# Cross-attention masks moved from TensorE to VectorE in a decoder layer, with work handed to GpSimd and a new instruction order

## The reference

```
x = x + self_attention(layernorm(x), w_qkv, w_out)             # 16 heads of 16, windows of 128:
                                                               # each window sees itself (causal) and the one before
x = x + cross_attention(layernorm(x), ctx, mask; Wq..Wo, biases)  # 77 context keys, mask[1024, 77]: 0 is -inf
x = x + ffn(layernorm(x))                                      # int8 fake quantisation of inputs, weights, hidden (704)
```

## Time and profile before

| | us |
|---|---|
| three timed executions | 696.09, 699.87, 700.06 (median 699.87) |
| the profiled execution | 695.62 |
| its span, first to last instruction | 693.5 |
| TensorE, VectorE, ScalarE, GpSimd busy | 607.9, 519.1, 406.6, 166.1 |
| attention ends (last values product) | about 553 |
| feed-forward begins (first int8 tokens) | about 582 |

### The profile page before, as it was taken

How to read it: one execution, slowest core, us unless ns; L and a number is a source line. 1 busy time by engine, 2 the same in 40 slices (tenths; PEclk the granted TensorE clock), 3 DMA queues, 4 the chain that set the end, 5 groups by cost and what they waited for, 6 DMA issues and landing times.

```text
span 693.5 us, 19987 instructions
## 1 busy us (share of the span) xinstructions
PE 607.9 (88%) x8020; PEld 393.6 (57%) x8020; DVE 519.1 (75%) x985; ACT 406.6 (59%) x602; POOL 166.1 (24%) x213
## 2 busy tenths in 40 slices
PE   2799999999999999999999999999989843877395
PEld 2556575867665766566757656576646432333173
DVE  6698877877787677757866966686697476699677
ACT  3345666775675547556555476544545715999682
POOL 2014332431344301320441033220120001455200
PEclk9999999999999999999999999999999966999789
DMA  7644133562344344246324353443473320000024
GB/s 258 182 153 134 42 122 110 143 155 66 111 136 112 104 117 104 71 138 165 114 52 145 79 145 102 113 112 93 101 216 98 75 48 1 0 1 1 0 92 153
DMA packets 58554, 72.17 MB, mean 104 GB/s; under 512 B 23979, under 2 KB 35423, under 8 KB 58463
## 3 DMA queue, kind: packets, MB, share of 16 engines
q1 hardware_dynamic: 54783, 68.92, 35.6%
q10 hardware_dynamic: 3680, 1.97, 1.1%
HBM read 17.74 MB, written 4.72 MB: 32 GB/s over the span
## 4 chain that ended last, share of the span: by engine, by line
PE 59%; DVE 19%; issue 6%; SPq 6%; DMA 5%; ACT 4%; ACTq 0%; POOL 0%; DVEq 0%; POOLq 0%
PE banks L484 38%; PE banks L664 7%; DVE mneg L1098 5%; PE banks L584 4%; PE banks L675 4%; SPq L417 2%; DVE tops L1282 2%; PE banks L528 2%; PE banks L729 1%; SPq L435 1%; DVE big L1276 1%; SPq L412 1%; DVE parts L1264 1%; DVE mneg L1102 1%; DMA out_dram<-oTs 1%
## 5 line engine op out<-in xcount | busy, mean ns | idle before, releaser
L484 PE MATMUL banks<-big 96*128 96x77 bf16 (+3 forms) x1344 | 157.7, 238 | 8.2 <-DVE mneg L1102 2.7
L1098 DVE TENSOR_REDUCE mneg<-banks 128x4 f32<-128x640 f32 (+3 forms) x128 | 126.9, 1019 | 38.7 <-PE banks L593 38.2
L484 PEld LDWEIGHTS banks<-big 99*128 99x128 bf16 (+2 forms) x1344 | 101.9, 101 | 75.2 <-issue 30.1
L1379 POOL TENSOR_SCALAR_AFFINE_SELECT big<-big 128x512 f32<-128x512 f32 x96 | 65.5, 683 | 230.1 <-ACT big L900 229.4
L900 ACT ACTIVATE big<-banks 128x1024 f32<-128x1024 f32 x96 | 96.9, 1028 | 38.9 <-PE banks L484 38.6
L484 PE MATMUL banks<-xnT,weights 128*128 128x512 f32 x192 | 92.4, 611 | 0.2 <-DVE mneg L1098 0.2
L584 PE MATMUL banks<-big 96*32 96x160 bf16 (+3 forms) x1792 | 70.8, 257 | 0.9 <-DVE mneg L1098 0.4
L904 ACT ACTIVATE big<-banks 77x1024 f32<-77x1024 f32 x48 | 47.6, 1021 | 26.5 <-PE banks L484 24.5
L1102 DVE TENSOR_REDUCE mneg<-banks 128x8 f32<-128x616 f32 x64 | 49.3, 790 | 14.6 <-PE banks L484 14.1
L664 PE MATMUL banks<-big 128*17 128x256 f32 x768 | 57.0, 382 | 0.2 <-ACT oe L913 0.2
L729 PE MATMUL banks<-oe,weights 128*128 128x512 bf16 x192 | 47.7, 395 | 10.1 <-DVE big L1276 4.4
(11 more groups left out here) (159 smaller groups left out, 1191.1 us busy)
## 6 DMA issues: line engine op xcount, KB each, us to landing
big<-parts SPq DMA_DIRECT2D x285, 128.0 KB, 2.5
oc<-sums SPq DMA_DIRECT2D x16, 512.0 KB
oTs<-oe SPq DMA_DIRECT2D x64, 64.0 KB, 2.5
out_dram<-oTs SPq DMA_DIRECT2D x16, 256.0 KB, 2.2
xs<-in_x_dram SPq DMA_DIRECT2D x3, 1024.0 KB, 6.0
big<-oe SPq DMA_DIRECT2D x32, 64.0 KB, 2.4
oTx<-oe SPq DMA_DIRECT2D x32, 64.0 KB, 2.4
xs<-in_x_dram SPq DMA_DIRECT2D x2, 512.0 KB, 6.3
```

The source lines that it names most:

```text
L484: return e.matmul(to[0:w], k[:, 0:w], q, start=start, stop=stop, skip_group_check=True)
L1098: e.tensor_reduce(M.rearrange("p (h c) -> p h c", h=4)[:, :, c], pair(p).rearrange("p j (s n) -> p (j s) n", s=2)[:, :, 0:160 + 32 * (c % 4)],
L1379: e.affine_select(out=P[:, :, 0:128], in_=P[:, :, 0:128], compare_op=ALU.is_ge, fill=0.0, base=0, pattern=[[0, 4], [1, 128]], channel_mult ...
```

## The change

1. `maskt` becomes f32 and holds a cap: 3e38 where the mask keeps a key, 0 where it doesn't. The two identity products are gone from each cross `score`. A new step `keep` (letter H), on VectorE, takes the minimum of the exponentials and the cap, and `val` waits for it instead of for ScalarE. The masks of the maxima stay as they are.
2. The step `split`'s third part goes from VectorE to GpSimd.
3. `scale` goes from VectorE to GpSimd for 15 of the 16 jobs.
4. For the last job the sums don't go through DRAM. VectorE multiplies the inverted sums into two tiles of 512 columns (`broad`), which TensorE multiplies by a matrix of zeros and ones (`heads`, made once by GpSimd in `pick`); VectorE then scales `oT` by the two banks. `store` and `widen` of that job are gone.
5. `ORDER` is a new string.

```
@@ maskt, once
-                    e.tensor_copy(maskt[0:KX, :], bank(p).bitcast(BF16)[0:KX, :]).then_inc(d_mask, 1)
+                    e.tensor_scalar(maskt[0:KX, :], bank(p).bitcast(BF16)[0:KX, :], 0.0, BIG, ALU.is_equal, ALU.mult
+                                    ).then_inc(d_mask, 1)
@@ TensorE, score of a cross job
-                        keep = maskt[0:KX, j * 256:j * 256 + 256].rearrange("p (a n) -> p a n", a=1)
                         for z in range(2):
                             for i in range(2):
-                                whole(bank(p, z)[0:KX, i * 256:i * 256 + 256], xks[r][0:99, 2 * z + i, :],
-                                       qs[r][0:99, 2 * z + i, j * 256:j * 256 + 256], i == 0, False, KX)
-                            t = whole(bank(p, z)[0:KX, :].rearrange("p (i n) -> p i n", i=2), identb[0:KX, 0:KX],
-                                       keep.to_broadcast([KX, 2, 256]), False, True, KX)
+                                t = whole(bank(p, z)[0:KX, i * 256:i * 256 + 256], xks[r][0:99, 2 * z + i, :],
+                                          qs[r][0:99, 2 * z + i, j * 256:j * 256 + 256], i == 0, True, KX)
@@ TensorE, val of a cross job
-                        e.wait_ge(a_exp, n_of["score", job, g, j])
+                        e.wait_ge(d_keep, n_of["keep", job, g, j])
@@ VectorE
-                elif k == "split":
...
-                    e.tensor_tensor(P[:, 2, :], rem[:, rem_at[s[1:]], :], P[:, 1, :], ALU.subtract).then_inc(d_p2, 1)
+                elif k == "keep":
+                    _, job, g, j = s
+                    P = pt[pt_at[job, g, j]][0:KX, :].rearrange("p (i n) -> p i n", i=4)
+                    e.wait_ge(a_exp, n_of["score", job, g, j])
+                    e.wait_ge(d_mask, 2)
+                    e.tensor_tensor(P, P, maskt[0:KX, j * 256:j * 256 + 256].rearrange("p (a n) -> p a n", a=1).to_broadcast(
+                        [KX, 4, 256]), ALU.min).then_inc(d_keep, 1)
-                elif k == "scale":
...
+                elif k == "broad":
+                    e.wait_ge(d_inv, len(JOBS))
...
+                    e.tensor_tensor(grown[:, s[1] * 512:s[1] * 512 + 512].rearrange("p (j n) -> p j n", j=8),
+                                    ls[:, 1, :].rearrange("p (a n) -> p a n", a=1).to_broadcast([128, 8, 64]),
+                                    group[:, 8 * s[1]:8 * s[1] + 8].rearrange("p (j a) -> p j a", a=1
+                                                                              ).to_broadcast([128, 8, 64]),
+                                    ALU.mult).then_inc(d_broad, 1)
+                elif k == "scale" and s[1] == JOBS[-1]:
...
+                    for half in range(2):
+                        to = oT[kind][f][:, half * 512:half * 512 + 512]
+                        e.wait_ge(t_broad, half + 1)
+                        e.tensor_tensor(to, to, bank(at_bank["broad", half][0]), ALU.mult).then_inc(d_scale, 1)
@@ TensorE, new
+                elif k == "broad":
+                    e.wait_ge(p_pick, 3)
+                    e.wait_ge(d_broad, s[1] + 1)
+                    whole(bank(p), heads, grown[:, s[1] * 512:s[1] * 512 + 512], True, True).then_inc(t_broad, 1)
@@ GpSimd, new
+                elif k == "scale":
...
+                    e.wait_ge(land_r, 32 * (n + 1))
+                    for g in range(2):
+                        e.wait_ge(land_o[g], 64 * (n + 1))
+                    e.tensor_tensor(oT[kind][f], oT[kind][f], oc[:, :], ALU.mult).then_inc(p_scale, 1)
+                elif k == "split":
+                    _, job, z, blk = s
+                    e.wait_ge(a_p1, n_of[s])
+                    P = parts[:, z, :, blk * 512:blk * 512 + 512]
+                    e.tensor_tensor(P[:, 2, :], rem[:, rem_at[s[1:]], :], P[:, 1, :], ALU.subtract).then_inc(p_p2, 1)
```

More of the change, by code:

```diff
@@ L22 @@
 NEG = -1.0e30
+BIG = 3.0e38
 EPS = 1e-5
@@ L29 @@
 AT = {j: n for n, j in enumerate(JOBS)}
+LAST_SELF = [j for j in JOBS if j[0] == "s"][-1]
 UNITS = {"s": NC, "x": 4}
@@ L67, in streams @@
         "s": [("score",) + unit for unit in units],
+        "H": [("keep",) + unit for unit in units if unit[0][0] == "x"],
         "v": [("val", job, g, j, j == UNITS[job[0]] - 1) for job, g, j in units],
@@ L72, in streams @@
         "i": [("invert", job) for job in JOBS],
-        "d": [("store", job) for job in JOBS],
-        "w": [("widen", job) for job in JOBS],
+        "d": [("store", job) for job in JOBS[:-1]],
+        "w": [("widen", job) for job in JOBS[:-1]],
+        "b": [("broad", half) for half in range(2)],
+        "P": [("pick",)],
         "x": [("scale", job) for job in JOBS],
@@ L132 @@
 WIDE = {"turned": 2, "max": 2, "score": 2, "up": 2}
-NARROW = {"turnw", "turnc", "masks", "keys", "qk", "v", "xkeys", "turnm", "out", "wturn", "turnx", "down", "dsc", "peak"}
+NARROW = {"turnw", "turnc", "masks", "keys", "qk", "v", "xkeys", "turnm", "out", "broad", "wturn", "turnx", "down", "dsc", "peak"}
 def banks_of(steps, count_of):
@@ L168, in build @@
         ks = [ring[:, r, 1] for r in range(4)]
-        fourth = sb("fourth", [128, 1024], F32)
-        pt = [big[:, 16384 + 1024 * i:17408 + 1024 * i] for i in range(3)] + [fourth[:]]
+        more = sb("more", [128, 1024], F32)
+        pt = [big[:, 16384 + 1024 * i:17408 + 1024 * i] for i in range(3)]
+        pt += [more[:, 1024 * i:1024 * i + 1024] for i in range(NPT - 3)]
         rem = big[:, 19456:20480].rearrange("p (i n) -> p i n", i=2)
@@ L387, in run_sync @@
                     for part, ready, n in ((0, a_p0, n_of["qk", job, z, 1]), (1, a_p1, n_of["split", job, z, 1]),
[L388 removed]
+                                           (2, p_p2, n_of["split", job, z, 1]))[:1 if s == first_keys else 3]:
                         e.wait_ge(ready, n)
@@ L414, in run_sync @@
                     else:
-                        e.wait_ge(d_p2, n_of["split", job, z, 1])
+                        e.wait_ge(p_p2, n_of["split", job, z, 1])
                         for rr in range(6):
@@ L446, in run_sync @@
                     if AT[job]:
-                        e.wait_ge(d_scale, AT[job])
+                        e.wait_ge(p_scale, AT[job])
                     else:
@@ L681, in run_tensor @@
                     e.wait_ge(ld_wo, 32)
-                    e.wait_ge(d_scale, scale_n((kind, b, 0), 1))
-                    e.wait_ge(d_scale, scale_n((kind, b, 1), c // 4))
+                    for f in range(2):
+                        n = AT[kind, b, f]
+                        e.wait_ge(*((p_scale, n + 1) if n < len(JOBS) - 1 else (d_scale, c // 4 + 1)))
                     for i in range(2):
@@ L756, in build @@
                 n_cross[s[1:]] = seen_cross
-        def scale_n(job, half):
-            n = AT[job]
-            return n + 1 + (half if n == len(JOBS) - 1 else 0)
         ffn = [("peak", 0)]
@@ L1073, in run_vector @@
                                                ).then_inc(d_rem, 1)
-                elif k == "split":
-                    _, job, z, blk = s
-                    e.wait_ge(a_p1, n_of[s])
-                    before = prior(job, lambda j: z == 0 or j[0] == "s")
-                    P = parts[:, z, :, blk * 512:blk * 512 + 512]
-                    e.tensor_tensor(P[:, 2, :], rem[:, rem_at[s[1:]], :], P[:, 1, :], ALU.subtract).then_inc(d_p2, 1)
                 elif k == "xkeys":
```

87 lines of the change are left out of this document (54 added, 33 removed).

## The result

The changed kernel takes 717.13 us (median, 709.34 to 720.97); the kernel before, measured beside it, 699.00. The ratio is 1.0226 with a 95% interval of [1.0184, 1.0269]: **slower by 2.3%**, where 684 us was forecast. The highest of the four runs after was in the slow state and counts in the median, but not in the ratio, so the loss is 16 us by the ratio and 18 by the medians. The profiled execution took 716.34 us (span 714.6), 20.7 over that of before.

A forecast was written before the change was run, and what follows sets the result against it. TensorE was taken to bound attention, VectorE its tail after the change. Start -3, middle -10, tail +6 and end -5, together -12 from the profiled 695.62 us, gave 684 us, range 667 to 702.

The forecast's parts named there:

- 212 to 455 us: Attention while own and cross jobs alternate: TensorE still bounds, 14.1 us less masks, 4 back for contention and later selects: -10.
- The tail, +6 (0 to +12): Only-cross attention, 455 to 553 us: VectorE becomes the bound with 99 us of work at 93% busy, +6 us.
- the first rival: All hidden: VectorE's 25 idle us of the tail take the minimums without loss, tail -10, 668 us; chance 0.18.
- VectorE's relief: 48 third-part subtractions (-32 us) and 15 scalings (-17 us) leave VectorE; GpSimd gets +61 and +38 us.
- The start: Until 212 us: VectorE -17.5 us, TensorE unchanged, slower splits take some back: -3 us (bounds -8 and +2).
- Part 4, the holds: VectorE and GpSimd operations with two SBUF inputs wait for each other: 11 us more on VectorE (bounds 0 and 41).
- The third rival: GpSimd and VectorE shut each other out at minimums and selects: 714 us, chance 0.12; sign: minimums' mean over 1.4 us.
- The Trainium skill's rule: GpSimd's SBUF interfaces are shared with VectorE, with contention for two SBUF inputs; the forecast said it speaks against this change.
- my second rival: Given back in the tail: tail +12, middle -5, start 0, end -4, TensorE's clock lower there: 699 us; chance 0.17.
- Casts' mean up from 317 ns: Sign in the profile after: the mean time of VectorE's casts rises from 317 ns.
- I am wrong if the mixed part doesn't shorten: Sign against the forecast: attention with alternating own and cross jobs, until 455 us, gets no shorter.
- The end, -5: Last sums through two products instead of DRAM: first out product at 560 instead of 565.01, -5 us (bounds -1 and -5.5).

The follow-up runs named there:

- half minimum: The change with each minimum on 77x512, half its columns, the other half unmasked, against the kernel before: 701.08 us, 1.0035.
- masks back: The change with its score masks back on TensorE and no minimum, splits and scalings still on GpSimd, against the kernel before: 704.59 us, 1.010.
- experiment 2: Parts of the change written into the old order, against the kernel before: end products 699.24 us, with third parts and scalings on GpSimd 708.94, all four parts 779.11.
- experiment 3: Idle VectorE work, shorter minimums or shared masks in the change's order, against the kernel before: idle minimums 718.93 us, half minimums 701.08, shared masks 703.28.
- load-only version: The change with masks on TensorE and an idle same-shape VectorE minimum in each minimum's place, nothing waiting for it, against the kernel before: 718.93 us, 1.0247.

## Why the prediction was wrong, step by step

- **The step that failed: "212 to 455 us ... TensorE still bounds; 14.1 less 4 for contention and later selects: -10".** Measured +11.3, which is 21 of the 33 us between forecast and result. Two terms of it failed. The 4 us for GpSimd's part was too small: with all masks on TensorE the move and the order cost 7.0 in the middle (5.8 for the move in the old order). And the 14.1 of relief didn't come: putting the masks on VectorE cost another 4.3. VectorE's busy time came out near the sum (192.0 against 185 and the holds), but I took 81% of a stage for "not the bound", while in jobs of 20 to 35 us it is full. With half the minimums' load the same relief of TensorE gives 7.8 us in the middle, so it can be had only while VectorE has room.
- **The tail, +6 (0 to +12).** Right in kind, a little over the upper bound in size, 12.2. VectorE bounds it (104.55 us of 110.3, 95%; 99 of work were forecast at 93%). "25 idle us of the tail" is what the first rival counted on: the half minimums found room for 22 us at a net price of 1.6 over masks back, the full ones, 37 us, cost 9.0.
- **VectorE's relief.** I counted 48 third parts and 15 scalings off VectorE as gains of its time and put little on GpSimd's side. In the old order they cost 9 to 10 us. The start came out at +2.4 in place of -3, and at +3.8 without minimums; GpSimd's queue does that rather than the order, which is likely from experiment 2, but not shown, since the new order doesn't stand VectorE in GpSimd's place. (The -17.5 of the start is 18.4 by its own terms, 22 x 0.68 and 3 x 1.15; nothing hangs on it.)
- **Part 4, the holds.** Normalisations rose by little (26.2 to 27.5 us) and casts fell (10.2 to 9.5), the minimums carry 7.5 us over 64 x 1.21: about 8 in place of 11. The third rival's sign, a mean over 1.4 us, did not show (1.33). Its 714 came near the measured time, but it asked for 0.36 us uncovered per minimum, and the holds are 0.12: luck in the number, not its mechanism.
- **The Trainium skill's rule** in "GPSIMD Engine Reference", section 1, that the SBUF interfaces are shared: the trace agrees, with 3.06 us in place of 1.21 for a minimum in a meeting. I used it for the price of the operations and not for the queue behind them.
- **The clock**, in my second rival, showed: between 212 us and the last mark its mean is 0.92 over 369.5 us, some 60 us at the half level, against 1.00 before. In the tail it costs little: the half minimum has a tail with 0.83 that is 7 us shorter. In the stretch from 287 to 349 us, where VectorE doesn't bound, it may be a part of the 5 us that experiment 3 finds; no run separates it from the link.
- **Signs:** GpSimd at 1.2 and 2.4 us, VectorE full in the tail with TensorE at 78%, and values products waiting for minimums (14.0 us in 11 waits) were right. "Casts' mean up from 317 ns" was wrong: it is 296. "I am wrong if the mixed part doesn't shorten": it didn't.
- **The end, -5.** Measured -4.9 behind the last mark, but that is luck. In the old order the products alone changed nothing (0.9991 to 1.0027), though the reciprocal behind the tiles made mark to end 131.5 us in place of 139.0: the mark moved, not the end. From the end of the last values product to the first out product I forecast 7 us in place of 12; it is 10, as the timeline of TensorE after shows (588.37 - 577.35 - 1.06). Two prices were missed: GpSimd's scaling of the job before holds the first multiply (2.26 us in place of 0.66), which I had only as a bound, and the two products take 3.75 us at the half clock, where I had 0.9 to 1.7. Another 2.3 us lie behind the first out product (128.5 us to the span's end before, 126.2 now).

```profile
577.35 1.06 PE L685 MATMUL banks<-more,big 77*17 77x256 f32 x8 [0.77 <-DVE more L1113]
584.47 3.75 PE L497 MATMUL banks<-big 128*128 128x512 f32 x4 [3.19 <-DVE big L1146]
588.37 0.75 PE L497 MATMUL banks<-weights,big 128*128 128x256 f32 x2
```

```profile
580.76 3.02 POOL L1411 TENSOR_TENSOR big<-big,oc 128x1024 f32<-128x1024 f32 x1 [31.03 <-DMA oc<-sums]
582.07 2.26 DVE L1146 TENSOR_TENSOR big<-ls,big 128x512 f32<-128x512 f32 x1
```

## What to carry to other kernels

Before moving work onto an engine, read its busy share in windows of 20 to 40 us, cut where the kernel's own marks lie, not in one of 243: VectorE's average of 79% hid jobs at 97 to 99%. Compare two versions between the same marks, never in the same microseconds, and look at more than one mark, since effects can cancel between two. Here relief for an engine that wasn't the bound (VectorE) brought nothing, and the queue of its new host had a price. In an order written by hand, undoing one part measures the order as much as the part; try an added operation as idle work nobody waits for, and in shorter sizes, since these two leave the order alone.

## What the runs showed of the hardware

- A hold between VectorE and GpSimd goes both ways and lasts to the end of the other's operation: a 1.21 us minimum took 3.06 beside a 2.39 us scaling, and the 1.27 us addition behind took 2.13. An operation of VectorE with one SBUF input (77x1024 reduction, 64 of them, 1.157 to 1.217 us each) was never held in a kernel with the same GpSimd operations, where the minimum with two inputs in its place went up to 2.68 us.
- GpSimd's 128x512 subtraction with a bf16 output took 1.16 us undisturbed (mean 1.19), its 128x512 operation with an f32 output 1.27, its 128x1024 f32 product 2.36; VectorE does the first in 0.71 (mean) and the last in 1.22.
- TensorE's granted clock went to the half level (1.2 of 2.4 GHz) seven times in the change's attention between 271 and 555 us, for 3.4 to 17.1 us at a time; the longest, 17.1 us, began 1.2 us after TensorE had stood for 1.66 us. Its price in time isn't isolated: from mark X0a to X0b the change took 62.1 us at 0.84 and the load-only version, whose values products wait for no minimum, 57.5 at 0.97.
